# Layer 0 of a four-layer graph network: the per-node constants of the low edges are gathered in the second pass's gather loop

## The reference

```python
def _hconv(x, W, b, src, dst):
    x = x @ W
    deg_n = segment_sum(ones, src, N_NODES)
    deg_e = segment_sum(ones, dst, N_HEDGES)
    Dinv = where(deg_n > 0, 1.0 / deg_n, 0.0)
    Binv = where(deg_e > 0, 1.0 / deg_e, 0.0)
    he = Binv[:, None] * segment_sum(x[src], dst, N_HEDGES)
    out = Dinv[:, None] * segment_sum(he[dst], src, N_NODES)
    return out + b
h = relu(_hconv(h, W1, b1, src, dst))
x = x + _hconv(h, W2, b2, src, dst)
```

## Time and profile before

| | us |
|---|---|
| median of 3 runs | 3221.45 |
| the three runs | 3214.99, 3221.45, 3222.52 |
| the profiled execution's own time | 3215.13 |
| its span, first to last instruction | 3213.3 |
| busy: TensorE matmul / VectorE / ScalarE / GpSimd | 2140.7 / 2130.8 / 1683.2 / 1601.0 |
| mean granted TensorE clock (share of 2.4 GHz) | 0.825 |

### The profile page before, as it was taken

How to read it: one execution, slowest core, us unless ns; L and a number is a source line. 1 busy time by engine, 2 the same in 40 slices (tenths; PEclk the granted TensorE clock), 3 DMA queues, 4 the chain that set the end, 5 groups by cost and what they waited for, 6 DMA issues and landing times. The chain is left out here.

```text
span 3213.3 us, 49191 instructions
## 1 busy us (share of the span) xinstructions
PE 2140.7 (67%) x10561; PEld 1506.1 (47%) x10561; DVE 2130.8 (66%) x8711; ACT 1683.2 (52%) x4589; POOL 1601.0 (50%) x1511
## 2 busy tenths in 40 slices
PE   3673333627775877877845787778866777773666
PEld 1232331425554766666632333334436666662555
DVE  5688323308885988888957777777726444451999
ACT  2493001217883666566646988898945444440222
POOL 3200556350005888888827655565507777774000
PEclk9797667869995777676767999998988887886999
DMA  2297323429998887787837999999966555542998
GB/s 68 87 371 318 63 34 75 128 33 291 323 324 268 250 246 243 243 248 245 247 91 216 288 291 288 284 294 281 278 167 201 181 185 184 183 151 90 305 325 284
DMA packets 494679, 696.61 MB, mean 217 GB/s; under 512 B 66363, under 2 KB 357398, under 8 KB 485932
## 3 DMA queue, kind: packets, MB, share of 16 engines
q1 hardware_dynamic: 416414, 511.30, 50.6%
q0 software_dynamic: 63360, 130.75, 15.2%
q10 hardware_dynamic: 14736, 52.96, 4.4%
HBM read 394.91 MB, written 327.18 MB: 225 GB/s over the span
## 5 line engine op out<-in xcount | busy, mean ns | idle before, releaser
L262 POOL DMA_INDIRECT xs<-x_d,table_src x400 | 384.5, 961 | 361.1 <-DVE x L1491 133.5
L262 POOL DMA_INDIRECT xs<-n_d,srcI x200 | 241.4, 1207 | 327.2 <-DVEq L1140 271.3
L262 POOL DMA_INDIRECT xd<-n_d,dstI x200 | 220.7, 1103 | 61.0 <-issue 53.6
L262 POOL DMA_INDIRECT xd<-x_d,table_dst x200 | 211.2, 1056 | 65.1 <-issue 64.8
L1705 POOL DMA_INDIRECT r_d<-rd,out_row x200 | 196.8, 984 | 61.5 <-issue 58.8
L1828 PE MATMUL bank<-xs,same 128*128 128x129 f32 x400 | 106.6, 356 | 129.3 <-DVE same L1770 64.9
L1646 PEld LDWEIGHTS bank<-nmsg,same 128*128 128x128 f32 x400 | 62.5, 196 | 265.6 <-ACT sums L1578 206.2
L1646 PE MATMUL bank<-nmsg,same 128*128 128x128 f32 x400 | 101.2, 336 | 126.8 <-ACT sums L1578 74.1
L457 POOL DMA_INDIRECT sum_d<-add,to x40 | 65.1, 1629 | 235.8 <-ACT add L654 225.4
L238 DVE RECIPROCAL rs<-root 128x4 f32<-128x4 f32 (+3 forms) x253 | 52.0, 205 | 188.1 <-ACT root L257 171.0
L257 ACT ACTIVATE root<-tmp,eps 128x4 f32<-128x4 f32 (+3 forms) x253 | 76.7, 303 | 189.4 <-DVE tmp L233 189.1
(11 more groups left out here) (383 smaller groups left out, 7294.3 us busy)
## 6 DMA issues: line engine op xcount, KB each, us to landing
n_d<-T SPq DMA_DIRECT2D x98, 528.0 KB, 3.7
nt<-n_d SPq DMA_DIRECT2D x49, 1056.0 KB, 7.2
r<-r_d SPq DMA_DIRECT2D x98, 520.0 KB, 5.5
bc<-dst_d SPq DMA_DIRECT2D x170, 256.0 KB, 4.7
r_d<-nv SPq DMA_DIRECT2D x49, 528.0 KB, 8.0
v_d<-nv SPq DMA_DIRECT2D x49, 528.0 KB, 7.7
nv<-v_d SPq DMA_DIRECT2D x49, 528.0 KB, 4.1
x_d<-x SPq DMA_DIRECT2D x100, 256.0 KB, 4.2
```

Of the source, the lines that this page charges most:

```text
L262: pool.indirect_dma_start(out=out, out_offset=None, in_=table, in_offset=bass.IndirectOffsetOnAxis(ap=index, axis=0)).then_inc(s, 16)
```

## The change

- The four gathers of `meta_d` rows, their copy of `ix` and the copy to `ms_all` leave the scatter loop of stage 0, with the waits on them.
- In the gather loop of stage 1 each gather of `sum1_d` rows is followed by a gather of `meta_d` rows by the same index column.
- `first_sums` waits for `ms_in` and reads its constants from `ms`; one small VectorE copy keeps the four M_DINV columns of a group in the new tile `dinv`, from which stage 1's `additions` reads them. `ms_all` is gone.
- GpSimd's wait for `meta_out` moves from ahead of the first scatter loop to ahead of stage 1's gather loop. Zeroing and the copy of `x` stay where they were.

```diff
--- before.py
+++ after.py
@@ -315,7 +315,7 @@
             to_all = sb("to_all", [P, NT], I32, c)
             dump = sb("dump", [P, G], F32, c)
             ms = sb("ms", [P, 2, G, 8], F32, c)
-            ms_all = sb("ms_all", [P, NT, 8], F32, c)
+            dinv = sb("dinv", [P, NT], F32, c)
             last_cols = sb("last_cols", [P, 2 * G], F32, c)
             weight = [W["W1"], W["W2"]]
 
@@ -326,9 +326,8 @@
                     "x_copied", "hot_ready", "lows_ready", "hot_used", "deg_ready", "root_ready", "totals_ready", "offsets_ps",
                     "meta_ready", "meta_out", "groups_ready", "cols_ready", "cols_ps", "set_up", "firsts_ready"))
             ms_in = [sem(f"ms_in{s}") for s in range(2)]
-            ms_ready = sem("ms_ready")
             q = [{n: sem(f"c{conv}_{n}") for n in (
-                "ix_ready", "mx_ready", "stats_link", "mixed", "rooted", "inverted", "scaled", "row_link", "h_ready", "mask_ready",
+                "ix_ready", "stats_link", "mixed", "rooted", "inverted", "scaled", "row_link", "h_ready", "mask_ready",
                 "sums_ps", "sums_in", "across_ps", "across_in", "reach_ready", "he_ps", "count_link", "binv_ready", "he_ready",
                 "combine_ready", "comb_ps", "later_link", "to_ready", "add_ready", "added", "landed", "last_cols_ready",
                 "last_ps", "last_in")} for conv in range(2)]
@@ -441,10 +440,13 @@
                             hold("pool", pool, e["ix_ready"], g + 1)
                             for j in range(G):
                                 gather(pool, er[:, s, j, :], t["x"] if conv == 0 else sum1_d, ix[:, s, j:j + 1], er_in[conv][s])
+                                if conv == 1:
+                                    gather(pool, ms[:, s, j, :], meta_d, ix[:, s, j:j + 1], ms_in[s])
+                        if conv == 1:
+                            pool.wait_ge(meta_out, 16)
                         bounded(pool, n, gathers)
                         if conv == 0:
                             pool.wait_ge(zeroed, 16 * (NN // (P * 28) + 1))
-                            pool.wait_ge(meta_out, 16)
                         else:
                             pool.wait_ge(x_copied, 16 * (NX // COPY))
 
@@ -458,14 +460,6 @@
                                                         out_offset=bass.IndirectOffsetOnAxis(ap=to[:, s, j:j + 1], axis=0),
                                                         in_=add[:, s, j, :], in_offset=None,
                                                         compute_op=ALU.add).then_inc(e["added"], 16)
-                            if conv == 0:
-                                nc.gpsimd.tensor_copy(ix[:, s, :], srcI[:, bass.ds(g * G, G)]).then_inc(e["mx_ready"], 1)
-                                hold("pool", pool, e["mx_ready"], g + 1)
-                                for j in range(G):
-                                    gather(pool, ms[:, s, j, :], meta_d, ix[:, s, j:j + 1], ms_in[s])
-                                hold("pool", pool, ms_in[s], pre_count(g, s, G))
-                                nc.gpsimd.tensor_copy(ms_all[:, bass.ds(g * G, G), :], ms[:, s, :, :]).then_inc(ms_ready, 1)
-                                hold("pool", pool, ms_ready, g + 1)
                             pool.wait_ge(e["added"], g * (16 * G) + 16 * G)
                             pool.sem_inc(e["landed"], 1)
                         pool.sem_inc(e["landed"], 2)
@@ -656,7 +650,7 @@
                             else:
                                 for j in range(G):
                                     last = nc.scalar.activation(add[:, s, j, :], comb_bank[s][:, j * P:(j + 1) * P], ACT.Copy,
-                                                                scale=ms_all[:, bass.ds(g * G + j, 1), M_DINV])
+                                                                scale=dinv[:, bass.ds(g * G + j, 1)])
                             last.then_inc(e["add_ready"], 1)
                         lagged(act, n, rows_of_edges, additions)
                     stages(0)
@@ -830,16 +824,17 @@
                             nc.vector.tensor_tensor(nb[:, s, :], neg[:, s, :], rs[:, s, :], ALU.mult).then_inc(e["scaled"], 1)
 
                         def first_sums(g, s):
-                            dve.wait_ge(ms_ready, g + 1)
+                            dve.wait_ge(ms_in[s], pre_count(g, s, G))
+                            nc.vector.tensor_copy(dinv[:, bass.ds(g * G, G)], ms[:, s, :, M_DINV])
                             for j in range(G):
                                 last = nc.vector.scalar_tensor_tensor(
-                                    out=er[:, s, j, :], in0=er[:, s, j, :], scalar=ms_all[:, bass.ds(g * G + j, 1), M_DINV],
+                                    out=er[:, s, j, :], in0=er[:, s, j, :], scalar=ms[:, s, j, M_DINV:M_DINV + 1],
                                     in1=R["b1"][:, :], op0=ALU.mult, op1=ALU.add)
                             last.then_inc(e["row_link"], 1)
                             dve.wait_ge(e["row_link"], g + 1)
                             for j in range(G):
                                 last = nc.vector.scalar_tensor_tensor(
-                                    out=er[:, s, j, :], in0=he_last[0][:, :], scalar=ms_all[:, bass.ds(g * G + j, 1), M_CHIGH],
+                                    out=er[:, s, j, :], in0=he_last[0][:, :], scalar=ms[:, s, j, M_CHIGH:M_CHIGH + 1],
                                     in1=er[:, s, j, :], op0=ALU.mult, op1=ALU.add)
                             last.then_inc(e["scaled"], 1)
 
```

## The result

| | before | after |
|---|---|---|
| median of the comparison's runs, us | 3217.99 (14 runs) | 3207.46 (14 runs) |
| profiled execution's own time, us | 3215.13 | 3210.24 |
| its span, us | 3213.3 | 3208.5 |
| busy: TensorE / VectorE / ScalarE / GpSimd, us | 2140.7 / 2130.8 / 1683.2 / 1601.0 | 2155.1 / 2130.7 / 1682.6 / 1602.5 |
| mean granted TensorE clock | 0.825 | 0.824 |

After over before is 0.9965, 95% interval [0.9953, 0.9977]: faster by 0.35%, or 11.3 us (7.4 to 15.1) of 3218. The forecast was -9.8 us.

What follows compares the result with a forecast made beforehand. Layer 0's scatter loop was held by a chain of waits, its gather loop by GpSimd's own stream; -59.8 + 48.1 + 1.9 = -9.8 us, from 3221.45 to 3211.6 us, range 3203 to 3223.

Steps and rivals of the forecast that it cites:

- The scatter loop: Stage 0 of layer 0: without index copy, gathers, their wait and copy, the stretch falls from 184.15 to 124.3 us, gain 59.8.
- The ring: Stage 0's scatter loop as a chain of waits: four scatters, GpSimd's work until `landed`, then 3.42 us to the next scatter.
- The landing: Completion of stage 0's adds, now bare: 2.2 us in six groups with loads beside them, 1.95 in the other four.
- The scatters: Forty scatters of stage 0: 65.1 us, with thirty gaps of 0.30 us 74.2 us for ten groups.
- From the last landing to the next loop: End of stage 0's scatter loop: 0.8 us from the last landing to the next loop's index copy.
- the last hand-over: Ahead of stage 0's last group: its scatter does not pass through VectorE, for which 0.9 us was taken.
- The gather loop: Stage 1: forty added gathers cost 51.0 us on GpSimd's stream, less 2.9 us of waits given back, so 48.1 us.
- The waits for `h`: GpSimd in stage 1's gather loop: 2.9 us of waiting, expected to vanish with groups of 11 us.
- The end of the loop: After stage 1's last gather, to the last `sumT`: from 11.1 to 13.0 us, cost 1.9 us, between 0 and 3.
- The first rival, the dear landing: Scatter loop: a new 3.6 us wait in six groups with loads, 8.4 us more, net -1.4 us; chance 0.18.
- The second rival, stretched gathers: Gather loop: VectorE's masks block added gathers, up to 20 us more, net +10.2 us; chance 0.08.
- The cheaper case: Both loops: landings all 1.94 us, loop end free, gathers at 0.941 us, net -14.6 us, 3206.9 us; chance 0.08.

Runs made afterwards that it cites:

- e1: Changed kernel without the added gathers of constants, which become a tile of ones: 3451.65 us, ratio to before 0.9848.
- e4: The changed kernel run again without an edit, in the first set of follow-up runs: 3489.15 us, ratio to before 0.9995.
- e11: Kernel before, its gathers kept in stage 0's scatter loop, two ahead of `landed` and two behind, collected two groups later; repeat in the third set: 3499.22 us, ratio 0.9852.

## Why the prediction was right

**The scatter loop.** Forecast -59.8, measured -61.8, and -61.9 by the means of four profiles. The ring was read rightly: four scatters, landing, 3.4 us, with groups of 12.68 us where I had 13.0 to 13.5. Four terms were off a little, and partly cancel. The landing took 2.09 us on average where I took 2.2 with loads beside, and 1.93 without. The scatters are cheaper than in the earlier trace rows, 63.1 us in all instead of 65.1: the first of a group averages 1.67 us instead of 1.84. From the last landing to the next loop it is shorter too: 2.27 us with the landing, where I had 1.95 + 0.8 = 2.75. Against me, the last hand-over was 4.46 instead of 2.85 us, from the two `bc` loads, which I had not looked for: in the kernel before they were issued 1.35 us ahead of a group's end, but the gathers covered the landing. That is the step left out: a transfer that stands beside a wait that was covered.

**The gather loop.** Forecast +48.1, measured +47.1, and +48.8 by the means of four profiles. The kernel without constants gives 49.6 us for the same loop by another way. The waits for `h` were gone in three of four profiles of the changed kernel, and 4.6 us in the fourth. The end of the loop is luck: +1.5 in the first pair where I had 1.9, but my starting point of 11.1 us is the shortest of the four profiles of before (11.1 to 14.5), and without the added gathers the same end takes 14.6 us (e1) where with them it takes 14.7 (e4). No run shows that the change costs anything there.

**The first rival, the dear landing,** rested on 3.60 us with loads 1.09 us ahead of the end. It did not happen in the loop, where the nearest load stands 3.2 to 4.8 us ahead; it did happen once, at the `bc` loads. The lengthening is real, its place was wrong. The Trainium skill, "DMA: Bandwidth & Descriptors", section on the anatomy of one DMA, gives a fixed cost of about 2.0 us and calls it nearly constant; the landings of 1.92 to 2.21 us agree with it, the one beside the `bc` loads, 4.46 less about 0.9 for the hand-over, does not.

**The second rival, stretched gathers,** needed 1.22 us a gather; they average 1.007, the longest 1.247. The instructions on `ms` in the changed kernel (ns min/median/max):

```profile
L262 POOL DMA_INDIRECT ms<-meta_d,ix x40: 942/947/1247, 451.6 to 558.3; - x40
```

The median is 0.947, so most meet nothing. Single blocks of 0.3 us are there, one per gather is not. The Trainium skill, "SBUF — State Buffer", section on a bandwidth-pool intuition that is wrong, has about 3100 ns for a DMA of GpSimd beside a VectorE copy; the longest gather of this loop took 1247.

**The cheaper case** had -14.6 us from a free end and short gathers. Layer 0 in the first pair came to -16.0, but not by these: 2.8 us of it lie behind the loops. I had set these stretches to nothing. The 1.6 us ahead of stage 1's first scatter are the spread of both kernels: that piece takes 19.4 to 19.8 us in the profiles where TensorE is busy 10.7 us in it, and 21.0 to 21.4 where it is busy 12.0 to 12.3, and either is seen in either kernel. The 1.2 us behind it come again: 113.4 to 114.3 us in the four profiles of the changed kernel, 114.4 to 115.8 in those of before. No run takes that piece apart, so its cause stays open. TensorE's granted clock in the scatter loop is higher in the changed kernel (0.70 to 0.72, where it was 0.64 to 0.66), but that loop does not wait for TensorE.

**The sum.** The medians say -10.5 us of 3218, the forecast was -9.8. That agreement is closer than its parts deserve: layer 0's stretch says -13.9 on the mean of four profiles each, of which the two terms that hold, -61.9 and +48.8, make -13.1; the first comparison's ratio says -7.4 to -15.1 us, and the four comparisons together spread wider still. A net of ten is the difference of two terms of sixty and fifty, each off by one or two us here.

## What to carry to other kernels

An engine that waits inside a ring, a loop in which each turn waits for the one before, pays for everything that is put between the last issue and the signal, but nothing for what fits into its idle time once nobody waits for the result; so before moving work out of a ring, look whether it can be collected a turn or two later, which was worth four times as much here (-55 us of layer 0 against -14). Price a move by both loops, each by what bounds it: the removal was worth more than the gathers' busy time, 61.8 for 39.0, because waits went with it, and the addition cost all of it and the gaps, 47 to 49, because it went to a loop held by that engine's own stream. When a covering step goes, ask for each other queue which transfer now falls on the uncovered wait.

## What was unexpected of the hardware

- The completion of accumulating scatters depends on what is issued near their end. In the four profiles of the changed kernel it took 1.91 to 2.28 us in the loop, with the nearest 256 KB load 3.1 us or more ahead of the end or none; one of e11 took 2.71 with a load 2.86 us ahead. For landing and hand-over of the last group it was 4.34 to 4.46 us with two 256 KB loads issued 0.7 to 1.6 us ahead of the last scatter's end (in the first profile 435.39 - 434.68 = 0.71), 3.78 with them 1.95 us ahead, and 2.92 with those loads held back.
- A gather issued behind the scatters does not delay their completion: with one at 406.65, the adds of the scatter that ended at 406.35 had landed by 408.30.
- Most gathers of 128 rows cost GpSimd 0.94 to 1.03 us, whether the row is 8 constants or 128 features: in the changed kernel's gather loop both have a median of 0.947 us.
- One kernel on different occasions differs behind layer 0 and hardly in it: medians from 3218 to 3545 us over the first comparison and chips 0, 2 and 4, layer 0's stretch from 393.5 to 397.8.
